# Attention value products as four 64x64 array tiles into two PSUM banks, with row sums of the second key tiles by accumulating DMAs

## The chip, the cores and the metric

The kernel runs on one core of one Trainium2 chip. The metric is device time in microseconds (us) of that core; the times below are medians over runs of the same kernel. The trace and the page come from one further execution, taken by the hardware profiler.

Engine names: PE is TensorE, DVE is VectorE, ACT is ScalarE, POOL is GpSimd, SP is SyncE. PEld stands for weight loads, which overlap with matmuls. L1001 is line 1001 of the kernel before.

## The reference

Two images of 64 channels and 96 x 96 pixels go through a convolution stage and a one-head attention over all N = 9216 pixels; nearly all of the time is spent in the second.

```python
h = group_norm1(x, n1_g, n1_b)
f = dwconv(h, w3, b3) + dwconv(h, w5, b5) + dwconv(h, w7, b7)
g = sigmoid(conv1x1(f, gate_w, gate_b))
x = x + conv1x1(f * g, proj_w, proj_b)
h = group_norm1(x, n2_g, n2_b)
q = conv1x1(h, q_w, q_b).reshape(B, C, N).transpose(0, 2, 1)
k = conv1x1(h, k_w, k_b).reshape(B, C, N)
v = conv1x1(h, v_w, v_b).reshape(B, C, N).transpose(0, 2, 1)
attn = softmax(einsum('bnc,bcm->bnm', q, k) * C ** -0.5, axis=-1)
out = einsum('bnm,bmc->bnc', attn, v)
return x + out.transpose(0, 2, 1).reshape(B, C, H, W)
```

## The kernel before

Per image the queries are cut into 18 blocks (j) of 512. A block goes over 72 tiles of 128 keys, taken as 36 pairs (p = 0 to 35, the two tiles of a pair are t = 0 and 1). For a pair, `scores` (L980) makes two 128x512 score tiles in two PSUM banks, from fp16 parts with 64 rows and 128 columns of weights at a time, so that two such products use the two halves of the array's rows. One ScalarE instruction (`exponentials`, L540) turns both tiles into exponentials in slot p of the ring E in SBUF, 8 pairs deep. `weigh` (L997) multiplies them by the values: 128 rows and 64 columns of fp32 weights per key tile, tile t = 0 into the upper 64 partitions of one bank (ACC_BANK, 6) and t = 1 into the lower 64. Each fp32 matmul is two records in the trace, one per pass over the 512 columns.

The softmax needs the sum of the exponentials per query. GpSimd adds up the first tiles of the pairs in accA (`add_a`, L466); VectorE adds up the second tiles in PSUM bank 7 (`add_b`, L800) and copies them out to accB at the block's end (`sums_out`). In the next block GpSimd adds accA and accB (`total`, L479), TensorE sums over partitions (`row_sums`, L1033), ScalarE copies the sums out, VectorE takes reciprocals in eight parts, GpSimd adds the two halves of the value products (pva, pvb), multiplies them by the reciprocals, and VectorE adds the residual (`write_out`). The value products are moved out of PSUM by three ScalarE copies of 64x256 (`move_pv`, L551, behind the exponentials of p = 1) and one VectorE copy (`move_last_pv`, L825, the first thing in a VectorE block).

The softmax also needs a bound of each row's maximum, for the block after: `visit` (L1049) makes maximum scores into two PSUM banks (MX_BANK) twice per two pairs, and VectorE reduces each to one column (`reduce_max`, L787), which frees the banks for the next visit. Near the block's end the maxima are spread over partitions by TensorE (`spread_maxima`, L1012), placed by ScalarE (`place_maxima`), and turned by GpSimd into a source, mseed (`fill_source`, L487, the first thing in a GpSimd block); `seed` (L578) on ScalarE then writes mseed into the score banks of every odd pair from 3 on, two pairs ahead, and the scores of that pair accumulate on it.

Every engine has one queue, in the order of the code, and waits for counting semaphores. On TensorE two pairs go in this order: visit(p), scores of p + 2, scores of p + 3 (behind the seed), visit(p + 1), weigh(p), weigh(p + 1). The row sums of the block before stand between weigh(6) and weigh(7), the spread of maxima between weigh(32) and weigh(33). The two score tiles of an even pair and of an odd pair each have their own two banks.

## Time and profile before

| | us |
|---|---|
| median of 2 runs | 2826.18 (2825.94 to 2826.41) |
| span of the profiled execution | 2823.7 |
| TensorE busy | 2759.1 (98%) |
| VectorE busy | 2501.6 (89%) |
| ScalarE busy | 2207.9 (78%) |
| GpSimd busy | 1823.3 (65%) |
| share of the 16 DMA engines, hardware queues | 6.1% |

The profile gives the busy time of an engine as the union of its instructions. Ends of matmuls are modelled and overlap the next start, so that the pace of TensorE is read from starts. The timeline merges neighbouring instructions of one line into one row with a count; a row's second number is the time from the first start to the last end.

### The profile page before, as it was taken

The numbers are of one execution on the slowest core, as the hardware profiler recorded it, in microseconds if no ns is written. First come the engines' busy times: TensorE is split into PE (matmuls) and PEld (weight loads), VectorE is DVE, ScalarE is ACT, GpSimd is POOL, SyncE is SP. The second block draws the span as 40 slices with busy tenths as digits, with TensorE's granted clock in tenths as the row PEclk, the third lists the DMA queues.
The fourth block names the chain that finished last, engine by engine and source line by source line (L and its number), as shares of the span: only waits on it lengthen the run. The fifth ranks groups of instructions, "written<-read, shape, count | busy, mean of one in ns | idle before, by whom it ended". The sixth has DMA issues, their size and how long they took to land.

```text
span 2823.7 us, 54475 instructions
## 1 busy us (share of the span) xinstructions
PE 2759.1 (98%) x19648; PEld 935.0 (33%) x19648; DVE 2501.6 (89%) x3164; ACT 2207.9 (78%) x2290; POOL 1823.3 (65%) x1479
## 2 busy tenths in 40 slices
PE   7899999999999999999988999999999999999999
PEld 4333333333333333333323333333333333333332
DVE  5689999999999999999758999999999999999994
ACT  4467888888888888888867788888888888888888
POOL 1346666666666666666754666666666666666666
PEclk9999999999999999999999999999999999999999
DMA  6103000000000000000000000000000000000000
GB/s 203 41 9 75 10 11 10 11 10 10 11 10 11 10 11 11 10 11 9 5 5 16 9 10 11 10 11 11 11 10 10 11 10 11 10 10 9 9 7 5
DMA packets 35768, 48.20 MB, mean 17 GB/s; under 512 B 7848, under 2 KB 33960, under 8 KB 34992
## 3 DMA queue, kind: packets, MB, share of 16 engines
q1 hardware_dynamic: 35504, 44.75, 6.1%
q8 instruction: 157, 2.57, 0.4%
q14 instruction: 107, 0.88, 0.1%
HBM read 16.41 MB, written 9.44 MB: 9 GB/s over the span
## 4 chain that ended last, share of the span: by engine, by line
PE 93%; DVE 4%; issue 1%; ACT 1%; POOL 0%; SPq 0%; DMA 0%; DVEq 0%; ACTq 0%; POOLq 0%
PE ps L1001 42%; PE ps L992 35%; PE ps L1008 12%; DVE mxp L791 3%; PE ps L1121 2%; PE ps L1036 1%; PE ps L1207 0%; PE ps L1148 0%; PE ps L1163 0%; DVE ps L807 0%; PE ps L1097 0%; PE ps L1017 0%; ACT arena L547 0%; DVE bn L898 0%; ACT ps L583 0%
## 5 line engine op out<-in xcount | busy, mean ns | idle before, releaser
L471 POOL TENSOR_TENSOR arena<-arena 128x512 f32<-128x512 f32 x1224 | 1558.8, 1274 | 792.6 <-ACT arena L547 713.7
L791 DVE TENSOR_REDUCE mxp<-ps 128x1 f32<-128x1024 f32 x1296 | 1575.5, 1220 | 171.6 <-PE ps L1008 139.9
L547 ACT ACTIVATE arena<-ps,bnd 128x1024 f32<-128x1024 f32 x1296 | 1372.7, 1110 | 416.0 <-PE ps L992 362.0
L1001 PE MATMUL ps<-arena,vals 128*64 128x512 f32 x5184 | 1268.2, 605 | 0.2
L992 PE MATMUL ps<-arena 64*128 64x512 f16 x7776 | 1051.8, 376 | 5.3 <-ACT ps L583 3.2
L807 DVE TENSOR_TENSOR ps<-ps,arena 128x512 f32<-128x512 f32 x1224 | 844.8, 690 | 68.1 <-ACT arena L547 67.3
L583 ACT ACTIVATE ps<-mseed 128x1024 f32<-128x1024 f32 x612 | 629.0, 1028 | 56.5 <-ACT arena L547 4.8
L1008 PE MATMUL ps<-arena,QM 64*128 64x512 f16 x2592 | 500.0, 383 | 18.2 <-DVE mxp L791 13.5
L992 PEld LDWEIGHTS ps<-arena 64*128 64x128 f16 x7776 | 375.2, 94 | 419.6 <-ACT arena L547 28.8
L1001 PEld LDWEIGHTS ps<-arena,vals 128*64 128x64 f32 x5184 | 310.8, 136 | 501.6 <-issue 337.5
L1008 PEld LDWEIGHTS ps<-arena,QM 64*128 64x128 f16 x2592 | 124.6, 93 | 738.8 <-DVE mxp L791 638.5
L992 PE MATMUL ps<-arena,one 64*128 64x512 f16 x1368 | 259.6, 376 | 0.0
L823 DVE RECIPROCAL rec<-rsum 128x32 f32<-128x32 f32 x280 | 95.2, 342 | 0.1
L992 PEld LDWEIGHTS ps<-arena,one 64*128 64x128 f16 x1368 | 66.7, 94 | 81.0
L490 POOL TENSOR_SCALAR mseed<-arena 128x512 f32<-128x512 f16 x36 | 53.6, 1490 | 34.2 <-ACT arena L576 31.4
L476 POOL TENSOR_TENSOR arena<-arena 128x512 f32<-128x512 f32 x36 | 45.9, 1274 | 35.0 <-ACT arena L547 35.0
L1121 PE MATMUL ps<-arena 32*24 32x384 f32 x1792 | 56.0, 540 | 12.5 <-issue 6.3
L524 POOL TENSOR_TENSOR arena<-arena 128x512 f16<-128x512 f32 x36 | 41.7, 1161 | 37.3 <-ACT arena L671 37.3
L1207 PE MATMUL ps<-f,wT 128*128 128x512 f32 x72 | 43.2, 698 | 4.9 <-ACT f L653 3.2
L485 POOL TENSOR_TENSOR accS<-arena 128x512 f32<-128x512 f32 x35 | 45.4, 1296 | 0.1
L638 ACT ACTIVATE arena<-ps,prm 128x512 f32<-128x512 f32 x18 | 12.3, 687 | 40.8 <-PE ps L1148 40.8
L514 POOL TENSOR_TENSOR f<-f,arena 128x512 f32<-128x512 f32 x18 | 22.7, 1273 | 32.7 <-ACT arena L638 32.7
(122 smaller groups left out, 667.4 us busy)
## 6 DMA issues: line engine op xcount, KB each, us to landing
arena<-arena SPq DMA_DIRECT2D x144, 64.0 KB, 2.0
arena<-in_x_rows SPq DMA_DIRECT2D x8, 816.0 KB, 9.8
xs<-in_x SPq DMA_DIRECT2D x4, 1152.0 KB, 15.6
f_scratch<-arena SPq DMA_DIRECT2D x32, 144.0 KB
f<-f_scratch SPq DMA_DIRECT2D x16, 288.0 KB, 9.9
QM<-arena SPq DMA_DIRECT2D x72, 64.0 KB, 2.0
xst<-arena SPq DMA_DIRECT2D x72, 64.0 KB, 1.9
out<-ot SPq DMA_DIRECT2D x72, 64.0 KB, 2.0
```

The costliest lines, as they stand in the source:

```text
L471: nc.gpsimd.tensor_tensor(accA[:, n % 2, :], accA[:, n % 2, :], e, ALU.add).then_inc(adda_free, 1)
L476: nc.gpsimd.tensor_tensor(accA[:, n % 2, :], E[:, slot_of(n % 2, 0), 0, :], E[:, slot_of(n % 2, 1), 0, :], ALU.add).then_inc(adda_free, 2)
L490: nc.gpsimd.tensor_scalar(mseed[:, n % 2, :], QS[:, n % 2, 2, :], ONE * C, None, ALU.mult).then_inc(mseed_ready, 1)
L547: nc.scalar.activation(flat(E[:, slot_of(n % 2, p), :, :]), flat(ps[:, S_BANK + 2 * buf:S_BANK + 2 * buf + 2, :]), ACT.Exp, scale=bnd[:, 6 ...
L583: nc.scalar.activation(ps[:, S_BANK + 2:S_BANK + 4, :], mseed[:, n % 2, :].unsqueeze(1).to_broadcast([P, 2, CH]), ACT.Copy).then_inc(seede ...
L791: nc.vector.reduce_max(flat(mxp[:])[:, v:v + 1], flat(ps[:, bank:bank + 2, :]), AX.X).then_inc(mx_free, 1)
L807: nc.vector.tensor_tensor(ps[:, SUM_BANK, :], ps[:, SUM_BANK, :], e, ALU.add).then_inc(addb_free, 1)
L823: nc.vector.reciprocal(rec[:, at], rsum[:, at]).then_inc(rec_ready, 1)
L992: a = nc.tensor.matmul(ps[:, S_BANK + 2 * (p % 2) + t, :], of[rows], QS[rows, par, part, :], start=(k == 0 and seeds is None), stop=(k == ...
L1001: a = nc.tensor.matmul(ps[C * t:C * t + C, ACC_BANK, :], V[:, p, t, :], E[:, slot_of(par, p), t, :], start=(p == 0), stop=(p == NPAIR - 1) ...
L1008: a = nc.tensor.matmul(ps[:, bank + t, :], QM[rows, half, qt * P:(qt + 1) * P], KH[rows, kc * CH:(kc + 1) * CH], start=True, stop=True)
L1121: a = nc.tensor.matmul(ps[GRP * h:GRP * h + WROWS, conv_bank(s) + g, 0:WN].rearrange("p (w x) -> p w x", x=W), bands[rows, k * KW + dx, :] ...
```

## The change

- `weigh` makes four products per pair instead of two: the 128 keys of a tile are split into two halves of 64 rows (r), so that each product has 64 rows and 64 columns. The halves r go to two banks, 6 and 7, and are added later.
- Bank 7 is therefore no longer free for the sums of second tiles. In blocks 0 to 16 of an image GpSimd issues 18 DMAs (`dump`), each of two pairs' second tiles (128 partitions x 1024 fp32, 512 KB), into two halves of accD in turn: the first of each half copies, the others add to what is there (`accum_op`). A dump waits on GpSimd's queue for the one two before it to have landed. They stand behind the adds of the pairs in DUMP_AFTER, the last two both behind p = 35. In block 17 VectorE still adds, in bank 4.
- VectorE adds accD together behind p = 6 of the next block (`sum_dumps`: one add of 128x1024, one of 128x512).
- The ring E has 12 pairs instead of 8, laid out so that second tiles of neighbouring pairs are contiguous. The exponential of a pair waits for the dump of the pair 12 earlier instead of for VectorE's add.
- The value products leave PSUM so: one ScalarE copy of 128x512 from bank 6 (`move_pv`, behind p = 1), one VectorE add of bank 7 to it (`add_pv`, first in VectorE's block), two ScalarE copies of 64x256 across partitions (`turn_pv`, behind p = 4), two VectorE adds of 64x256 (`sum_pv`, behind p = 10, instead of GpSimd's add).
- The row sums move from p = 6 to p = 12, GpSimd's total from the block's start to behind p = 8, its final product from p = 28 to 33, the reciprocals to p = 17 to 31, `write_out` from p = 32 to 35.

```diff
-NSLOT = 8
+NSLOT = 12
-ROW_SUMS = 6
+ROW_SUMS = 12
+LASTS = NBLK - 1
+DUMP_AFTER = (8, 9, 11, 12, 14, 15, 17, 18, 20, 21, 23, 25, 27, 29, 31, 33, 35, 35)
+NDUMP = len(DUMP_AFTER)
+DUMPS_SUMMED = 6
...
+            def dump(b, j, g):
+                n, k = blk(b, j), g % 2
+                at = slot_of(n % 2, 2 * g)
+                pool.wait_ge(e_ready, NPAIR * n + 2 * g + 3)
+                if g >= 2:
+                    pool.wait_ge(dumped[k], dumps_before(b, j, g))
+                    pool.dma_start(accD[:, k, :], E[:, 1, at:at + 2, :].rearrange("p s c -> p (s c)"), accum_op=ALU.add
+                                   ).then_inc(dumped[k], 16)
+                else:
+                    if n:
+                        pool.wait_ge(accb_out, n)
+                    pool.dma_start(accD[:, k, :], E[:, 1, at:at + 2, :].rearrange("p s c -> p (s c)")).then_inc(dumped[k], 16)
...
                 fill_source(n)
                 first_a(n)
-                if j:
-                    total(n - 1)
                 for p in range(2, NPAIR):
                     add_a(n, p)
-                    if j and p == 12:
-                        pool.wait_ge(acc_free, 4 * n)
-                        if n > 1:
-                            pool.wait_ge(o_ready, n)
-                        nc.gpsimd.tensor_tensor(pvt[:], pva[:], pvb[:], ALU.add).then_inc(pv_summed, 1)
-                    if j and p == 28:
+                    if j < LASTS:
+                        for g in range(NDUMP):
+                            if DUMP_AFTER[g] == p:
+                                dump(b, j, g)
+                    if j and p == DUMPS_SUMMED + 2:
+                        total(n - 1)
+                    if j and p == 33:
                         pool.wait_ge(rec_ready, RECS * n)
...
                 act.wait_ge(adda_free, m + 1)
-                act.wait_ge(addb_free, m + 1)
-                nc.scalar.activation(flat(E[:, slot_of(n % 2, p), :, :]),
-                                     flat(ps[:, S_BANK + 2 * buf:S_BANK + 2 * buf + 2, :]),
+                if m >= NSLOT:
+                    was, q = divmod(m - NSLOT, NPAIR)
+                    b, j = divmod(was, NBLK)
+                    if j < LASTS:
+                        act.wait_ge(dumped[q // 2 % 2], dumps_before(b, j, q // 2) + 16)
+                    else:
+                        act.wait_ge(addb_free, NPAIR * b + q + 1)
+                nc.scalar.activation(E[:, :, slot_of(n % 2, p), :],
+                                     ps[:, S_BANK + 2 * buf:S_BANK + 2 * buf + 2, :],
...
-                for k, h in parts:
-                    nc.scalar.activation((pva, pvb)[k][C * h:C * h + C, :],
-                                         ps[C * k:C * k + C, ACC_BANK, h * HCH:(h + 1) * HCH], ACT.Copy).then_inc(acc_free, 1)
+                nc.scalar.activation(flat(pvc[:]), ps[:, ACC_BANK, :], ACT.Copy).then_inc(acc_copied, 1)
+
+            def turn_pv(n):
+                act.wait_ge(acc_free, n + 1)
+                for h in (0, 1):
+                    nc.scalar.activation(pvx[C * h:C * h + C, :], pvc[C - C * h:2 * C - C * h, h, :], ACT.Copy).then_inc(pv_turned, 1)
...
+            def sum_dumps(b, j):
+                n = blk(b, j)
+                for k in (0, 1):
+                    dve.wait_ge(dumped[k], dumps_before(b, j + 1, 0))
+                chain(nc.vector.tensor_tensor(accD[:, 0, :], accD[:, 0, :], accD[:, 1, :], ALU.add))
+                if n:
+                    dve.wait_ge(sum_ready, n)
+                nc.vector.tensor_tensor(accB[:], accD[:, 0, 0:CH], accD[:, 0, CH:2 * CH], ALU.add).then_inc(accb_out, 1)
...
-                nc.vector.tensor_copy(pvb[C:P, :], ps[C:P, ACC_BANK, HCH:CH]).then_inc(acc_free, 1)
+            def add_pv(n):
+                dve.wait_ge(acc_copied, n + 1)
+                nc.vector.tensor_tensor(flat(pvc[:]), ps[:, ACC_BANK + 1, :], flat(pvc[:]), ALU.add).then_inc(acc_free, 1)
...
-                    if p + 1 < NPAIR:
-                        add_b(n, p + 1)
+                    if j == LASTS and p + 1 < NPAIR:
+                        add_b(b, n, p + 1)
+                    if j and p == 10:
+                        sum_pv(n - 1)
+                    if j and p == DUMPS_SUMMED:
+                        sum_dumps(b, j - 1)
...
                 for t in (0, 1):
-                    a = nc.tensor.matmul(ps[C * t:C * t + C, ACC_BANK, :], V[:, p, t, :], E[:, slot_of(par, p), t, :],
-                                         start=(p == 0), stop=(p == NPAIR - 1), skip_group_check=True)
+                    for r in (0, 1):
+                        rows = slice(C * r, C * r + C)
+                        a = nc.tensor.matmul(ps[C * t:C * t + C, ACC_BANK + r, :], V[rows, p, t, :],
+                                             E[rows, t, slot_of(par, p), :], start=(p == 0), stop=(p == NPAIR - 1),
+                                             skip_group_check=True)
...
                     if p == 0 and not first:
-                        pe.wait_ge(acc_free, 4 * n)
+                        pe.wait_ge(acc_free, n)
```

## Rows read from the trace of the kernel before

**Rows 1.** The page: its first line, and the chain that ended last by engine.
```profile
span 2823.7 us, 54475 instructions
...
PE 93%; DVE 4%; issue 1%; ACT 1%; POOL 0%; SPq 0%; DMA 0%; DVEq 0%; ACTq 0%; POOLq 0%
```

**Rows 2.** Timeline, a steady period: start us, length us, engine, line, operation, count.
```profile
703.13 1.94 PE L1001 MATMUL ps<-arena,vals 128*64 128x512 f32 x8
...
703.57 2.69 POOL L471 TENSOR_TENSOR arena<-arena 128x512 f32<-128x512 f32 x2 [1.23 <-ACT arena L547]
...
704.59 1.03 ACT L583 ACTIVATE ps<-mseed 128x1024 f32<-128x1024 f32 x1
...
705.00 0.39 PE L1008 MATMUL ps<-arena,QM 64*128 64x512 f16 x2
...
705.43 1.23 DVE L791 TENSOR_REDUCE mxp<-ps 128x1 f32<-128x1024 f32 x1
...
705.87 0.38 PE L992 MATMUL ps<-arena,one 64*128 64x512 f16 x2
...
706.74 0.38 PE L1008 MATMUL ps<-arena,QM 64*128 64x512 f16 x2
...
707.05 1.51 PE L1001 MATMUL ps<-arena,vals 128*64 128x512 f32 x6
```

**Rows 3.** Timeline of TensorE around the row sums of two neighbouring blocks.
```profile
687.94 0.60 PE L1036 MATMUL ps<-accS,ones 128*64 128x256 f32 x4
...
759.13 0.60 PE L1001 MATMUL ps<-arena,vals 128*64 128x512 f32 x2
759.56 0.60 PE L1036 MATMUL ps<-accS,ones 128*64 128x256 f32 x4
```

**Rows 4.** Timeline of TensorE, one stretch of the convolution, 16 array tiles.
```profile
83.32 0.92 PE L1121 MATMUL ps<-arena 32*24 32x384 f32 x32
```

**Rows 5.** Timeline of TensorE between the images, three array shapes in turn.
```profile
1450.75 0.60 PE L1001 MATMUL ps<-arena,vals 128*64 128x512 f32 x2
1451.28 1.98 PE L1148 MATMUL ps<-f,wT 128*128 128x512 f32 x4
1453.19 0.65 PE L1036 MATMUL ps<-accS,ones 128*64 128x256 f32 x4
```

**Rows 6.** The page's groups: count, busy us, mean ns, idle before and its releaser.
```profile
L807 DVE TENSOR_TENSOR ps<-ps,arena 128x512 f32<-128x512 f32 x1224 | 844.8, 690 | 68.1 <-ACT arena L547 67.3
...
L485 POOL TENSOR_TENSOR accS<-arena 128x512 f32<-128x512 f32 x35 | 45.4, 1296 | 0.1
```

**Rows 7.** Timeline around a block's boundary.
```profile
739.78 0.60 ACT L576 ACTIVATE arena<-ps 128x512 f16<-128x512 f32 x1
...
741.68 1.49 POOL L490 TENSOR_SCALAR mseed<-arena 128x512 f32<-128x512 f16 x1
...
744.04 1.03 ACT L583 ACTIVATE ps<-mseed 128x1024 f32<-128x1024 f32 x1
...
744.84 0.43 DVE L830 COPY pvb<-ps 64x256 f32<-64x256 f32 x1
...
745.00 0.76 ACT L556 ACTIVATE pva<-ps 64x256 f32<-64x256 f32 x2
...
746.58 0.39 PE L1008 MATMUL ps<-arena,QM 64*128 64x512 f16 x2
```

**Rows 8.** Timeline of SP's queue: two DMAs issued.
```profile
741.07 1.12 SPq L363 DMA_DIRECT2D QM<-arena  x2
```

**Rows 9.** Groups of GpSimd by line, columns as in the page's groups.
```profile
L508 POOL TENSOR_TENSOR pvt<-pvt,rec 128x256 f32<-128x256 f32 x34 | 24.9, 732 | 0.0
```

**Rows 10.** The page's DMA issues: count, KB each, median us to landing.
```profile
arena<-in_x_rows SPq DMA_DIRECT2D x8, 816.0 KB, 9.8
...
QM<-arena SPq DMA_DIRECT2D x72, 64.0 KB, 2.0
```

**Rows 11.** Windows: busy us of each engine, TensorE's clock, DMA share, GB/s.
```profile
10.00:30.00 20.00, 13.73 (x217) 9.28 (x210) 9.45 (x31) 14.81 (x20) 0.00 (x0) 1.00 1.06 309
```

More of the change, by code:

```diff
@@ L147, in program @@
         accS = sb("accS", [P, CH])
-        pva = sb("pva", [P, HCH])
-        pvb = sb("pvb", [P, HCH])
+        accD = sb("accD", [P, 2, 2 * CH])
+        pvc = sb("pvc", [P, 2, HCH])
+        pvx = sb("pvx", [P, HCH])
         pvt = sb("pvt", [P, HCH])
@@ L237, in program @@
         accb_out = sem("accb_out")
+        dumped = [sem("dumped0"), sem("dumped1")]
         sum_ready = sem("sum_ready")
@@ L242, in program @@
         pv_summed = sem("pv_summed")
+        acc_copied = sem("acc_copied")
         acc_free = sem("acc_free")
+        pv_turned = sem("pv_turned")
         xst_ready = [sem("xst_ready0"), sem("xst_ready1")]
@@ L292, in pair0, with dumps_before @@
             return NPAIR * blk(b, j)
+        def dumps_before(b, j, g):
+            return 16 * (NDUMP // 2 * (LASTS * b + j) + g // 2)
         block = ctx.enter_context(nc.Block())
@@ L526, in _ @@
                     attend(b, j)
-                n = blk(b, NBLK - 1)
                 if b + 1 < B:
-                    total(n)
-                else:
-                    pool.wait_ge(acc_free, 4 * (n + 1))
-                    pool.wait_ge(o_ready, n + 1)
-                    nc.gpsimd.tensor_tensor(pvt[:], pva[:], pvb[:], ALU.add).then_inc(pv_summed, 1)
+                    total(blk(b, NBLK - 1))
         @block.scalar
@@ L594, in attend @@
                     if p == 1 and j:
-                        move_pv(n - 1, ((0, 0), (0, 1)))
-                        act.wait_ge(acc_free, 4 * n - 1)
-                        move_pv(n - 1, ((1, 0),))
+                        move_pv(n - 1)
+                    if p == 4 and j:
+                        turn_pv(n - 1)
                     if p == NPAIR - 3 and j + 1 < NBLK:
@@ L639, in _ @@
                                          bias=prm[:, GB:GB + 1]).then_inc(sig_ready, 1)
-                    if b and c in (1, 2):
-                        move_pv(blk(b, 0) - 1, ((c - 1, 0), (c - 1, 1)))
+                    if b and c == 1:
+                        move_pv(blk(b, 0) - 1)
+                    if b and c == 4:
+                        turn_pv(blk(b, 0) - 1)
                     if b and c == 3:
@@ L677, in _ @@
                     move_pv(blk(b, NBLK - 1))
+                    turn_pv(blk(b, NBLK - 1))
         @block.vector
@@ L853, in attend @@
                 if j:
-                    move_last_pv(n - 1)
+                    add_pv(n - 1)
                 for p in range(NPAIR):
@@ L872, in attend @@
                     if j:
-                        if 11 <= p < 11 + 2 * RECS and p % 2:
-                            reciprocals(n - 1, (p - 11) // 2)
-                        if p == 32:
+                        if ROW_SUMS + 5 <= p < ROW_SUMS + 5 + 2 * RECS and p % 2:
+                            reciprocals(n - 1, (p - ROW_SUMS - 5) // 2)
+                        if p == 35:
                             write_out(b, j - 1)
-                sums_out(n)
+                if j == LASTS:
+                    sums_out(b, n)
             joint_kernel()
@@ L910, in _ @@
                         x1_stats(c - 1)
+                    if b and c == 2:
+                        add_pv(blk(b, 0) - 1)
                     if b and c in (4, 5):
@@ L959, in _ @@
             n = blk(B - 1, NBLK - 1)
+            add_pv(n)
+            sum_pv(n)
             dve.wait_ge(rs_ready, n + 1)
```

46 lines of the change are left out of this document (22 added, 24 removed).

## The prediction

> **What bounds the kernel now.** I read the page first: the span, and the chain that ended last. 93% of that chain is TensorE [rows 1]: the span is a queue of matmuls, and work on other engines counts only where a matmul waits for it.
>
> Next the timeline of a steady stretch [rows 2]. One period treats two pairs of key tiles and lasts 707.05 - 703.13 = 3.92 us. TensorE goes without a pause from the value products (L1001) to maximum scores A (L1008, 705.00), scores (L992), maximum scores B (706.74) and value products again. The other engines have slack, but not everywhere:
> - VectorE's maximum over A runs from 705.43 to 706.66, and B, which overwrites the same two banks, starts at 706.74. Whatever delays that maximum, or stands long on VectorE between it and the next one, stops TensorE.
> - ScalarE's seed ends at 705.62; it is needed by the second half of the scores, which starts at 705.87. Slack 0.25 us.
> - GpSimd spends 2.69 us of 3.92 on its two adds, 1.345 us a pair against a pace of 1.96.
>
> Then one whole block of 36 pairs: from one block's row-sum matmuls to the next, 759.56 - 687.94 = 71.62 us [rows 3]. 18 x 3.92 = 70.56 of it is steady, so today's block boundary costs about 1 us. Of the 36 blocks 34 issue dumps, and 34 begin behind a block of the same image.
>
> **What the four tiles do.** The same 512 columns pass the array twice per matmul; today the two 64-column halves run side by side, 0.43 us a pass, 759.13 to 759.56 [rows 3]. Quarter tiles need the same passes if all four run side by side. The convolution says they do: 32 records of 16 tiles, two passes each, fit in 0.92 us [rows 4]. So the passes themselves gain nothing.
>
> What could be gained is the change of array shape. In each period L1001's four passes take 1.87 us up to 705.00, which is 4 x 0.43 + 0.15, and B to L1001 takes 0.31 where a plain pass takes (706.74 - 705.00) / 8 = 0.22 [rows 2]: about 0.25 us in all. I read it as 0.10 at each change and 0.05 for a first weight load: L1036 takes 0.65 us behind a change of shape and 0.60 without one [rows 3, 5]. Today rows (64 to 128) and columns (128 to 64) both change; afterwards only columns do. The trace has changes of columns alone, back to back [rows 5]: from L1001 (128x64) to L1148 (128x128) a pass takes 0.53 instead of 0.43, and L1148's four passes before L1036 (128x64) take 1.91, 0.19 over 4 x 0.43 for a change and a first weight load. So a change of columns alone costs 0.10 too, and I take the gain as 0, bounds 0 and 0.25 us a period (4.5 us a block).
> No row shows the pair 64x128 to 64x64 itself. The Trainium skill (TensorEngine Tiling (Array Packing), Tiling Modes) says that a change of tiling mode, unlike a change of tile, drains the engine, and lists 64x128 and 64x64 as different modes; by it the gain is 0.
>
> Two insertions get worse. Row sums and the spread of maxima stay 128x64 and today stand inside value products without a gap. Now each is a change to and fro: 2 x (2 x 0.10 + 2 x 0.05 for first loads) = **0.6 us a block** (below: 0, if changes of rows alone were free).
>
> **VectorE.** It loses 34 x 34 of its adds on L807, 0.69 us each [rows 6]. As TensorE does not wait for them, that gives 0. It gets sum_dumps after the maximum of p = 6, which is an A: a 128x1024 add and, behind a semaphore, a 128x512 add. No such add is in the trace; by the maximum over 1024 [rows 2] and L807 they take 1.23 + 0.06 + 0.69. The next maximum would end near 705.00 + 4.7, where the next A wants it by 3.92: **0.8 us a block** (below: 0, were the dumps' sum slid into slack). Two 64x256 adds after p = 10, under 0.9 us by the 0.43 of L830 [rows 7], fit where the old add was.
>
> **ScalarE.** turn_pv, two 64x256 copies (0.76 us, as the two of L556 [rows 7]), stands after p = 4, between two exponentials and ahead of the next seed. 0.76 against 0.25 of slack: **0.5 us a block** (bounds 0, if the exponentials can start earlier, and 0.8).
>
> **GpSimd and the boundary.** This is the largest term. 18 dumps a block are new on GpSimd's queue. The trace has no DMA from GpSimd; X is the time for which one holds it. SP issues two halves of 64 partitions in 1.12 us [rows 8]; a dump covers 128 partitions, so I take X = 1.12. Bounds: 0.56, one issue, below (0, were it all off the engine), and above 1.4, an estimate: a quarter more, since the target is also read.
> The Trainium skill (DMA: Bandwidth & Descriptors, Latency and other measured facts) has about 1 us to the first byte from GpSimd against about 0.6 from SP. By X = 1.0 the time would be 3,014 us.
>
> From p = 8 to 35 GpSimd has 28 adds x 1.345 = 37.7, the total (1.3) and the final product (0.7) [rows 6, 9] and 16 dumps before the last two: 39.7 + 16 X against 28 x 1.96 = 54.9. It ends the block late by 16 X - 15.2 = 2.7 us. Then two dumps, both after p = 35, stand ahead of the next block's fill_source: 2 X = 2.2. The last dump waits for the one two before it to land. A 64 KB transfer lands in 2.0 us [rows 10] and the loads at the start move 309 GB/s [rows 11], so 512 KB lands in about 3.7, or 5.4 if reading the target doubles it; GpSimd does 4.9 us of other work meanwhile: 0 to 0.5, taken as 0.3.
> So fill_source ends 5.3 us later than the 743.17 of today, L490 [rows 7], and the seed behind it, today at 744.04, waits. What is late next: seed 1.03, then the new move_pv (128x512, 0.60 as L576), then add_pv on VectorE (0.69), which stands ahead of the maximum over A (1.23), which B needs. With hops of about 0.05 B starts 3.8 us after fill_source ends; today it starts at 746.58. TensorE stops for 743.17 + 5.3 + 3.8 - 746.58 = **5.7 us a block**. If fill_source were not late at all, the longer chain alone (move_pv after the seed that ends at 745.07, then add_pv, where today L830 takes 0.43 beside ScalarE's copies) puts B at 747.7: 1.1 us, the bound below.
> The ring grows from 8 to 12 pairs, so the exponential's wait for a dump, issued four to eleven pairs ahead (7.8 us or more), is covered by a landing of under 5.4 us; with that cover gone TensorE would stop here too (second rival).
>
> **Sum.** 0.6 + 0.8 + 0.5 + 5.7 = 7.6 us, x 34 = 258 us. At the end of the program two copies and an add become a chain, about 2 us, and as much between the images. 2823.7 + 258 + 4 = 3,086 for the span; the median of the runs lies 2.5 above the profiled span: 3,088 us. With X = 0.56: (0.6 + 0.8 + 0.5 + 1.8) x 34 = 126, 2,956 us; with X = 1.4: 12.6 x 34 = 428, 3,258 us.
>
> **Rivals.**
> *The change of shape disappears*, because rows stay split in two. For it: only columns differ now. Against it: [rows 5]. It gives 36 x 4.5 = 162 us back. With X = 0.56: 2826 - 162 + 130 = 2,794 us, no change by 2%. But a faster TensorE leaves GpSimd 28 x 1.835 = 51.4 us, so that it is late from X = 0.73 on; at X = 1.12 the time is near 3,040. It decides (not slower by 2%) below X = 0.85; to be faster by over 2% the charges at p = 4 and 6 must be hidden as well.
> *The accumulating transfers are the bound.* 18 of them in 54.9 us on two chains allow a landing of 6.1 us each. The 816 KB loads, many at a time, land in 9.8 [rows 10]; at 9.8 the block would grow by 9 x 9.8 - 54.9 = 33 us, some 3,950 us; at 7 by 8 us and the 1.9 of the other terms, about 3,170.
> *The four tiles don't run together.* The passes would double: 18 x 1.72 x 36 = 1,115 us, about 3,940 us. Against it: [rows 4].
> *The boundary is better hidden than I count*: X near 0 and sum_dumps in slack: (0.6 + 1.1 + 0.5) x 34 = 75, 2,905 us.
>
> **How the numbers follow.** Forecast 0.56; shape change gone 0.14; transfers the bound 0.13; tiles not together 0.03; boundary hidden 0.14. The predicted time is the forecast's. The range takes in X from 0.56 to 1.4, the hidden boundary and the first rival at X = 0.56, and leaves out its faster part, most of the transfer case and the doubled passes: 2,790 to 3,280 us. A measurement of this kernel tells about 2%. Faster by over 2%: half of the first rival, 0.07. Within 2%: a part of the same rival and of the hidden case, 0.13. Slower: 0.80.
>
> **What the profile would show.** Right: L1001's passes at 0.43 us in groups of four tiles, with 0.10 still at each change; gaps on both sides of the row sums; GpSimd's L490 late and the seed waiting for it; TensorE idle some 5 us before the second maximum scores of each block, released by the maximum behind add_pv; a shorter stop after p = 6. Wrong: a steady period of 3.67 us; L490 as early as now; a dump that GpSimd is done with in 0.3 us; exponentials waiting for transfers.

## The result

| | before | after |
|---|---|---|
| median, us | 2826.18 (2825.94 to 2826.41) | 3034.35 (3020.39 and 3048.30) |
| span of the profiled execution, us | 2823.7 | 3046.6 |
| TensorE busy | 2759.1 (98%) | 2835.0 (93%) |
| VectorE busy | 2501.6 (89%) | 1956.6 (64%) |
| GpSimd busy | 1823.3 (65%) | 2302.1 (76%) |
| a block, us (median) | 71.61 (28 blocks) | 76.75 (12 blocks at full clock); 78.42 (16 blocks with a stretch of half clock) |

The blocks are the second to the fifteenth of each image. The changed kernel is slower: the ratio of the times is 1.0737 with a 95% interval of 1.062 to 1.0854. The forecast was 3,088 us, in a range of 2,790 to 3,280.

Lines of the changed kernel: value products L1058, maximum scores L1066, scores L1047, row sums L1094, maximum L827, exponentials L576, seed L617, fill_source L519, move_pv L585, add_pv L874, turn_pv L591, sum_dumps L850 and L853, GpSimd's adds L486, dumps L506 (plain) and L501 (accumulating). In the experiments they are shifted by a few lines.

The page of after: first line, busy time, and the chain that ended last by engine (compare [rows 1]).

```profile
span 3046.6 us, 63708 instructions
...
PE 2835.0 (93%) x24832; PEld 948.9 (31%) x24832; DVE 1956.6 (64%) x2081; ACT 2218.5 (73%) x2288; POOL 2302.1 (76%) x2056
...
PE 69%; DVE 10%; POOL 7%; issue 6%; ACT 6%; DMA 1%; ACTq 0%; SPq 0%; POOLq 0%; DVEq 0%
```

VectorE has lost more than a fifth of its work, and yet its share of the chain has grown from 4% to 10%; TensorE's has fallen from 93% to 69%. Where VectorE stands now counts more than how much it does.

Timeline of before, the first maximum scores at the two ends of a boundary period and of a period with row sums.

```profile
744.67 0.39 PE L1008 MATMUL ps<-arena,QM 64*128 64x512 f16 x2
...
748.77 0.39 PE L1008 MATMUL ps<-arena,QM 64*128 64x512 f16 x2
...
756.60 0.39 PE L1008 MATMUL ps<-arena,QM 64*128 64x512 f16 x2
...
760.95 0.39 PE L1008 MATMUL ps<-arena,QM 64*128 64x512 f16 x2
```

They take 748.77 - 744.67 = 4.10 us and 760.95 - 756.60 = 4.35 us.

Timeline of after, TensorE in one steady period and around the row sums (start us, length us, engine, line; compare [rows 2, 3]).

```profile
502.29 0.39 PE L1066 MATMUL ps<-arena,QM 64*128 64x512 f16 x2
...
504.33 1.95 PE L1058 MATMUL ps<-arena,vals 64*64 64x512 f32 x16
...
506.21 0.39 PE L1066 MATMUL ps<-arena,QM 64*128 64x512 f16 x2
...
509.28 0.65 PE L1094 MATMUL ps<-accS,ones 128*64 128x256 f32 x4
...
510.88 0.39 PE L1066 MATMUL ps<-arena,QM 64*128 64x512 f16 x2
```

The steady period is 506.21 - 502.29 = 3.92 us, as before. Sixteen records of quarter tiles take 1.95 us, as eight records of two tiles took: all four run side by side, and nothing is gained. The period with the row sums is 510.88 - 506.21 = 4.67 us.

Timeline of after around the boundary of [rows 7] (in brackets: idle before, and what ended it).

```profile
474.92 0.88 POOL L501 DMA_DIRECT2D accD<-arena  x1
...
476.04 0.87 POOL L501 DMA_DIRECT2D accD<-arena  x1 [0.24 <-issue]
...
476.99 1.49 POOL L519 TENSOR_SCALAR mseed<-arena 128x512 f32<-128x512 f16 x1
...
478.14 0.39 PE L1066 MATMUL ps<-arena,QM 64*128 64x512 f16 x2
...
478.51 1.03 ACT L617 ACTIVATE ps<-mseed 128x1024 f32<-128x1024 f32 x1 [1.09 <-POOL mseed L519]
...
479.47 0.58 ACT L585 ACTIVATE pvc<-ps 128x512 f32<-128x512 f32 x1
...
480.08 0.69 DVE L874 TENSOR_TENSOR pvc<-ps,pvc 128x512 f32<-128x512 f32 x1 [2.09 <-ACT pvc L585]
480.69 1.21 DVE L827 TENSOR_REDUCE mxp<-ps 128x1 f32<-128x1024 f32 x1
...
481.96 0.39 PE L1066 MATMUL ps<-arena,QM 64*128 64x512 f16 x2 [1.46 <-DVE mxp L827]
...
484.16 0.39 PE L1066 MATMUL ps<-arena,QM 64*128 64x512 f16 x2
```

This is the forecast's chain, link by link: dumps, fill_source, seed, move_pv, add_pv, maximum, second maximum scores. The period lasts 484.16 - 478.14 = 6.02 us. The wait ahead of the last dump, 0.24 here, is for the dump two before it to land: the last dump starts 0.56 us behind that landing in 30 of the 34 blocks. In 11 of the 34 blocks it is 0.8 to 1.7 us, in nine of them because that transfer landed 5.4 to 6.3 us after its issue instead of 4.8, and fill_source and the stop come later by about as much.

Timeline of after behind p = 4 and p = 6.

```profile
486.59 0.86 ACT L591 ACTIVATE pvx<-pvc 64x256 f32<-64x256 f32 x2
...
489.85 0.82 PE L1047 MATMUL ps<-arena 64*128 64x512 f16 x6 [0.51 <-ACT ps L617]
...
494.27 1.22 DVE L850 TENSOR_TENSOR accD<-accD 128x1024 f32<-128x1024 f32 x1
...
495.19 1.43 POOL L486 TENSOR_TENSOR arena<-arena 128x512 f32<-128x512 f32 x1 [1.68 <-ACT arena L576]
...
495.52 1.65 DVE L853 TENSOR_TENSOR arena<-accD 128x512 f32<-128x512 f32 x1
...
498.36 0.39 PE L1066 MATMUL ps<-arena,QM 64*128 64x512 f16 x2 [1.67 <-DVE mxp L827]
```

turn_pv makes the seed late. sum_dumps' second add, 128x512, takes 1.65 us beside an add of GpSimd, where L807 of the same size took 0.69 [rows 6]; TensorE then stands for 1.67 us.

The page's groups and DMA issues of after (count, busy us, mean ns; KB each, median us to landing), and two of its waits (in total, times, longest).

```profile
L501 POOL DMA_DIRECT2D accD<-arena x544 | 496.8, 914 | 34.9 <-ACT arena L576 11.4
...
L506 POOL DMA_DIRECT2D accD<-arena x68 | 40.9, 602 | 36.6 <-DVE arena L853 36.6
...
accD<-arena POOLq DMA_DIRECT2D x612, 512.0 KB, 4.8
...
POOL arena L486 <- ACT arena L576: 422.9, 444, 5.8
...
ACT arena L576 <- DMA accD<-arena: 4.7, 2, 4.0
```

One thing the forecast didn't have: behind many of the boundary stops TensorE's clock is half. Timeline of after in a later block, then windows over the same stretch (busy us of each engine, granted clock, DMA share, GB/s).

```profile
713.04 0.39 PE L1066 MATMUL ps<-arena,QM 64*128 64x512 f16 x2 [1.46 <-DVE mxp L827]
713.36 3.59 PE L1058 MATMUL ps<-arena,vals 64*64 64x512 f32 x16
```

```profile
709.50:713.30 3.80, 1.19 (x10) 0.35 (x8) 1.82 (x2) 3.62 (x5) 2.41 (x3) 1.00 0.95 194
713.40:716.60 3.20, 3.20 (x18) 0.76 (x16) 1.22 (x1) 0.86 (x1) 1.35 (x2) 0.50 0.10 27
716.90:720.80 3.90, 3.90 (x38) 1.28 (x34) 2.45 (x2) 2.55 (x4) 1.27 (x1) 1.00 0.00 0
```

Behind 3.80 us in which TensorE worked for 1.19, the granted clock is 0.50, that is 1.2 instead of 2.4 GHz, and the sixteen products take 3.59 us instead of 1.95. (In this block the last dump waited for 1.01 us, so that its stop is 0.9 us longer than the one shown above.) The page's span has 25 such stretches against 5 before; 16 of the 28 blocks of the first table have one.

**Where a block's time went.** The table takes each block apart by the starts of its first maximum scores: 18 periods a block, medians over blocks with full clock, us.

| period with | before | after | difference |
|---|---|---|---|
| the boundary | 4.10 | 6.03 | +1.93 |
| turn_pv (p = 4) | 3.92 | 4.62 | +0.70 |
| sum_dumps (p = 6) | 3.92 | 5.66 | +1.74 |
| the row sums | 4.35 | 4.67 | +0.32 |
| the spread of maxima | 4.20 | 4.49 | +0.29 |
| the 13 others, together | 51.12 | 51.28 | +0.16 |
| block | 71.61 | 76.75 | +5.14 |

5.14 x 34 = 175 us. The 20 additional half-clock stretches at about 1.67 (78.42 - 76.75) are 33. That is 208 of the 223 us between the spans. About 11 more are the longer stops of the blocks whose last dump waited longer; the rest lies in blocks with longer half-clock stretches, in the block during which the second image is loaded, and at the ends.

### The profile page after: what moved, and what is told of

The parts are those of the page before. It is cut to its first block, busy times and chain, and to the rows that moved or that the text cites. A ratio compares the mean times of both kernels' runs of the same rounds, so it can differ in the third digit from the quotient of the medians.

```text
span 3046.6 us, 63708 instructions
## 1 busy us (share of the span) xinstructions
PE 2835.0 (93%) x24832; PEld 948.9 (31%) x24832; DVE 1956.6 (64%) x2081; ACT 2218.5 (73%) x2288; POOL 2302.1 (76%) x2056
## 4 chain that ended last, share of the span: by engine, by line
PE 69%; DVE 10%; POOL 7%; issue 6%; ACT 6%; DMA 1%; ACTq 0%; SPq 0%; POOLq 0%; DVEq 0%
PE ps L1058 31%; PE ps L1047 24%; PE ps L1066 9%; DVE mxp L827 6%; POOL arena L486 3%; ACT arena L576 3%; DVE arena L853 2%; POOL mseed L519 2%; PE ps L1179 2%; ACT ps L617 1%; DVE accD L850 1%; POOL accD L501 1%; DMA accD<-arena 1%; ACT pvx L591 1%; DVE pvc L874 1%
## 5 line engine op out<-in xcount | busy, mean ns | idle before, releaser
L827 DVE TENSOR_REDUCE mxp<-ps 128x1 f32<-128x1024 f32 x1296 | 1579.9, 1223 | 857.6 <-PE ps L1066 856.5
L486 POOL TENSOR_TENSOR arena<-arena 128x512 f32<-128x512 f32 x1224 | 1642.3, 1342 | 490.0 <-ACT arena L576 422.9
L576 ACT ACTIVATE arena<-ps,bnd 128x1024 f32<-128x1024 f32 x1296 | 1379.5, 1111 | 571.0 <-PE ps L1047 559.2
L1058 PE MATMUL ps<-arena,vals 64*64 64x512 f32 x10368 | 1310.1, 616 | 0.6 <-DVE pvc L874 0.6
L1047 PE MATMUL ps<-arena 64*128 64x512 f16 x7776 | 1054.8, 377 | 49.5 <-ACT ps L617 45.9
L617 ACT ACTIVATE ps<-mseed 128x1024 f32<-128x1024 f32 x612 | 628.9, 1028 | 101.1 <-POOL mseed L519 50.1
L1066 PE MATMUL ps<-arena,QM 64*128 64x512 f16 x2592 | 503.7, 385 | 117.7 <-DVE mxp L827 113.0
L501 POOL DMA_DIRECT2D accD<-arena x544 | 496.8, 914 | 34.9 <-ACT arena L576 11.4
L1047 PEld LDWEIGHTS ps<-arena 64*128 64x128 f16 x7776 | 373.6, 94 | 480.1 <-issue 96.1
L1058 PEld LDWEIGHTS ps<-arena,vals 64*64 64x64 f32 x10368 | 330.8, 134 | 522.4 <-issue 356.4
L1066 PEld LDWEIGHTS ps<-arena,QM 64*128 64x128 f16 x2592 | 125.3, 93 | 847.0 <-DVE mxp L827 686.0
L1047 PE MATMUL ps<-arena,one 64*128 64x512 f16 x1368 | 259.9, 376 | 0.0
L1047 PEld LDWEIGHTS ps<-arena,one 64*128 64x128 f16 x1368 | 66.8, 94 | 81.5 <-issue 0.8
L843 DVE TENSOR_TENSOR ps<-ps,arena 128x512 f32<-128x512 f32 x68 | 47.6, 699 | 59.4 <-ACT arena L576 57.8
L874 DVE TENSOR_TENSOR pvc<-ps,pvc 128x512 f32<-128x512 f32 x36 | 24.9, 691 | 91.9 <-ACT pvc L585 91.9
L519 POOL TENSOR_SCALAR mseed<-arena 128x512 f32<-128x512 f16 x36 | 54.4, 1512 | 33.8 <-ACT arena L610 31.4
L506 POOL DMA_DIRECT2D accD<-arena x68 | 40.9, 602 | 36.6 <-DVE arena L853 36.6
L853 DVE TENSOR_TENSOR arena<-accD 128x512 f32<-128x512 f32 x34 | 54.2, 1593 | 1.2
L491 POOL TENSOR_TENSOR arena<-arena 128x512 f32<-128x512 f32 x36 | 45.6, 1266 | 6.7 <-ACT arena L576 3.9
```

Of the source, the lines that this page charges most:

```text
L486: nc.gpsimd.tensor_tensor(accA[:, n % 2, :], accA[:, n % 2, :], e, ALU.add).then_inc(adda_free, 1)
L501: pool.dma_start(accD[:, k, :], E[:, 1, at:at + 2, :].rearrange("p s c -> p (s c)"), accum_op=ALU.add).then_inc(dumped[k], 16)
L519: nc.gpsimd.tensor_scalar(mseed[:, n % 2, :], QS[:, n % 2, 2, :], ONE * C, None, ALU.mult).then_inc(mseed_ready, 1)
L576: nc.scalar.activation(E[:, :, slot_of(n % 2, p), :], ps[:, S_BANK + 2 * buf:S_BANK + 2 * buf + 2, :], ACT.Exp, scale=bnd[:, 6:7]).then_in ...
L617: nc.scalar.activation(ps[:, S_BANK + 2:S_BANK + 4, :], mseed[:, n % 2, :].unsqueeze(1).to_broadcast([P, 2, CH]), ACT.Copy).then_inc(seede ...
L827: nc.vector.reduce_max(flat(mxp[:])[:, v:v + 1], flat(ps[:, bank:bank + 2, :]), AX.X).then_inc(mx_free, 1)
```

## The experiments

Theory: the tiles give TensorE nothing, and the loss is a sum of places where another engine's new work makes TensorE wait. Rivals: the tiles do gain, and the stops hide it; or the load of the transfers, or of GpSimd, is what costs, wherever the work stands.

### Two tiles again

```diff
-                    for r in (0, 1):
-                        a = nc.tensor.matmul(ps[C * t:C * t + C, ACC_BANK + r, :], V[rows, p, t, :],
+                    a = nc.tensor.matmul(ps[C * t:C * t + C, ACC_BANK, :], V[:, p, t, :],
...
-                nc.vector.tensor_tensor(flat(pvc[:]), ps[:, ACC_BANK + 1, :], flat(pvc[:]), ALU.add).then_inc(acc_free, 1)
+                nc.vector.tensor_tensor(flat(pvc[:]), ps[:, ACC_BANK, :], flat(pvc[:]), ALU.max).then_inc(acc_free, 1)
```

> The kernel after, with the value products back as two 128x64 tiles into bank 6; add_pv takes a maximum of bank 6 with its own copy, so that its wait and its cost stay. Theory (the change of shape costs the same for 64x64 tiles, so the tiles give the steady period nothing and only make the two insertions of 128x64 products dearer): steady period 3.92 us as now, the periods with the row sums and the spread of maxima 0.3 and 0.5 us shorter, 0.85 us a block, 36 blocks, some 30 us below the kernel after: about 3,005 us. Rival (four tiles gain something that the new stops hide): the steady period grows to about 4.1 us and the time stays or rises. Rival (quarter tiles are themselves slower, by loads or by writing two banks): the steady period falls below 3.9 and the time by 60 us or more.

Measured: 3035.27 us (3032.51 to 3039.27), 1.0744 of before. The steady period stays 3.92; the row sums and the spread are 4.35 and 4.20 again, to the digit those of before. But the boundary grows from 6.03 to 6.32: the 0.29 saved just ahead of it is waited out there, since GpSimd's queue comes no earlier. A block is 76.28, so 0.47 less, and the span has 27 half-clock stretches. The 30 us that the theory expected don't show, and the times can't tell the two kernels apart; the periods can, and they bear out that the tiles give the steady period nothing.

### fill_source first

```diff
                 fill_source(n)
+                if j:
+                    for g in (NDUMP - 2, NDUMP - 1):
+                        dump(b, j - 1, g)
                 first_a(n)
```

> The kernel after, with the last two dumps of a block moved behind fill_source of the next block. Theory (fill_source is late by two dumps of 0.88 us on GpSimd's queue, and the seed, move_pv, add_pv and the maximum wait in a row behind it): fill_source ends up to 1.75 us earlier, the first cycle of a block falls from about 6.0 to about 5.0 us (the longer chain move_pv, add_pv stays), about 1 us a block, 34 us; and if the half-clock stretches that follow the boundary stop are caused by its length, most of them go too, another 0 to 40 us: 2,960 to 3,000 us. Rival (the chain move_pv, add_pv alone makes the stop, fill_source was in time): the first cycle stays near 6.0 and the time near 3,030 us. Rival (the transfers themselves load the memory): the same, no change.

Measured: 2967.26 us (2967.11 to 2968.72), 1.0506 of before. Timeline of this kernel's boundary:

```profile
474.23 1.49 POOL L519 TENSOR_SCALAR mseed<-arena 128x512 f32<-128x512 f16 x1
...
475.78 1.81 POOL L501 DMA_DIRECT2D accD<-arena  x2
...
476.68 1.03 ACT L620 ACTIVATE ps<-mseed 128x1024 f32<-128x1024 f32 x1
...
477.32 0.39 PE L1069 MATMUL ps<-arena,QM 64*128 64x512 f16 x2
...
480.14 0.39 PE L1069 MATMUL ps<-arena,QM 64*128 64x512 f16 x2 [0.92 <-DVE mxp L830]
```

fill_source now starts 3.09 us ahead of the first maximum scores instead of 1.15, and the seed waits for nothing. The boundary takes 5.02 us: 1.01 of its 1.93 was the two dumps ahead of fill_source, 0.92 is the longer chain through move_pv and add_pv. And 6 half-clock stretches are left in the whole span, about as many as before. So a move that shortens one stop by 1 us gave 67 us, and 80 between the two spans: 34 from the stop, some 32 from 19 half-clock stretches less, and about 11 from the last dump's longer waits, which now stand behind fill_source.

### turn_pv behind the seeds

```diff
-                    if p == 4 and j:
-                        turn_pv(n - 1)
+                    if p in (5, 7) and j:
+                        turn_pv(n - 1, ((p - 5) // 2,))
```

> The kernel after, with turn_pv's two copies moved from between the exponentials and the seed of p = 4, 5 to behind the seeds of p = 5 and p = 7, one each, where ScalarE is idle for 0.68 us. Theory (the copies make the seed late): the third cycle of a block falls from 4.62 to 3.93 us, 0.7 us a block, 24 us less: about 3,010 us. Rival (the work only moves and stops the array one period later, since ScalarE has no room): 0 to 5 us.

Measured: 3007.92 us (3004.00 to 3012.30), 1.0646 of before. The period of 4.62 is 3.93, a block 76.05, and no other period moved: as forecast. The span has 21 half-clock stretches.

### sum_dumps in three

```diff
-                    if j and p == DUMPS_SUMMED:
-                        sum_dumps(b, j - 1)
+                    if j and p in (DUMPS_SUMMED - 4, DUMPS_SUMMED - 2, DUMPS_SUMMED):
+                        sum_dumps(b, j - 1, (p - DUMPS_SUMMED + 4) // 2)
```

> The kernel after, with sum_dumps cut into three adds of 128x512, one each behind the maxima over A of p = 2, 4 and 6, where GpSimd runs no add. Theory (two adds in a row hold VectorE past the next maximum, and the second, 1.65 us beside a GpSimd add instead of 0.69, suffers from what the two engines share): each add takes about 0.7 us, the cycle of 5.66 us falls to 3.93, 1.7 us a block, 58 us less: about 2,975 us. Rival (the add is slow for its operands, whoever runs beside it): each of the three takes 1.2 to 1.65 us, three cycles of about 4.3 us take the place of the one, and the gain is 0.6 us a block, 20 us.

Measured: 3075.79 us (3072.55 to 3078.02), 1.089 of before: slower than the changed kernel. Timeline behind p = 6 and p = 10:

```profile
496.40 0.68 DVE L856 TENSOR_TENSOR arena<-accD 128x512 f32<-128x512 f32 x1
...
503.63 1.27 POOL L486 TENSOR_TENSOR arena<-arena 128x512 f32<-128x512 f32 x1
...
504.25 3.08 DVE L884 TENSOR_TENSOR pvt<-pvc,pvx 64x256 f32<-64x256 f32 x2
...
505.48 1.56 POOL L486 TENSOR_TENSOR arena<-arena 128x512 f32<-128x512 f32 x1
...
507.37 1.22 DVE L827 TENSOR_REDUCE mxp<-ps 128x1 f32<-128x1024 f32 x1
508.65 0.39 PE L1069 MATMUL ps<-arena,QM 64*128 64x512 f16 x2 [1.98 <-DVE mxp L827]
```

The three adds take 0.68, 0.82 (median over both lines of L852) and 0.68 us, and the period of 5.66 is 3.93: that part is as the theory has it, and the operands alone are not slow. But without the stop at p = 6 GpSimd stands elsewhere in its order when VectorE reaches sum_pv behind p = 10. sum_pv's two adds of 64x256, 0.99 us together in after, take 3.08: the first ends at 505.17, 0.27 behind GpSimd's add that began at 503.63, the second 0.29 behind the one that ended at 507.04. TensorE stands for 1.98 us; this period is now 5.97, and behind it the clock is half in 21 of the 31 blocks that have this stop (43 half-clock stretches in the span). The loss has moved, as the rival says, but to the next pair of adds that meet.

### The moves together, sum_pv clear of GpSimd's adds

```diff
-DUMP_AFTER = (8, 9, 11, 12, 14, 15, 17, 18, 20, 21, 23, 25, 27, 29, 31, 33, 35, 35)
+DUMP_AFTER = (9, 10, 11, 12, 14, 15, 17, 18, 20, 21, 23, 25, 27, 29, 31, 33, 35, 35)
...
-                    if j and p == DUMPS_SUMMED + 2:
+                    if j and p == DUMPS_SUMMED + 4:
                         total(n - 1)
...
-                    if j and p == 10:
+                    if j and p == 8:
                         sum_pv(n - 1)
```

besides the three edits above.

> The kernel after with the three moves together (last dumps behind fill_source; turn_pv behind the seeds of p = 5 and 7; sum_dumps as three adds behind p = 2, 4, 6), and sum_pv from behind p = 10 to behind p = 8, with the first two dumps and GpSimd's total one to two adds later, so that no GpSimd add runs beside sum_pv. Theory (the loss is a sum of places where one engine's new work makes TensorE wait, and two-operand adds of VectorE stand still while a GpSimd add or dump runs): periods of 3.93 us at turn_pv, sum_dumps and sum_pv, 5.02 at the boundary, 4.67 and 4.49 at the two insertions of 128x64 products; block 73.2 to 73.5 us against 71.6 before, no half-clock stretches: about 2,885 us. Rival (the load of the transfers or of GpSimd as such, whose stop turns up somewhere else as it did when sum_dumps alone was moved): a block of 75 us or more, over 2,940 us.

Measured: 2907.42 us (2903.38 to 2908.84), 1.0289 of before. The block is 73.30 us, with 3.93 at turn_pv, sum_dumps and sum_pv, 5.02 at the boundary, 4.67 and 4.49 at the insertions: every period is the theory's, and 6 half-clock stretches remain. The time is 22 us above it. Timeline of this kernel in the block during which SyncE loads the second image:

```profile
249.49 1.22 SPq L340 DMA_DIRECT2D f<-f_scratch  x2
...
265.22 0.69 DVE L855 TENSOR_TENSOR accD<-accD 128x512 f32<-128x512 f32 x1 [13.76 <-DMA accD<-arena]
```

That block takes 89.70 us, 16.4 more than the others, because VectorE waits 13.76 us for dumps to land while the loads are under way, which makes one period 13.5 us longer, and the next is 2.9 longer at half clock (that the loads are the cause is read from the time alone; it wasn't tried apart); the other blocks are 0.25 above their median on average, 7 us in all. 57 + 16 + 7 = 80 of the 82 us over before. So the transfers do cost something, in waits for their landing.

### The tiles alone

```diff
-                    a = nc.tensor.matmul(ps[C * t:C * t + C, ACC_BANK, :], V[:, p, t, :], E[:, slot_of(par, p), t, :],
+                    for r in (0, 1):
+                        rows = slice(C * r, C * r + C)
+                        a = nc.tensor.matmul(ps[C * t:C * t + C, ACC_BANK + r, :], V[rows, p, t, :],
...
-                    if p + 1 < NPAIR:
-                        add_b(n, p + 1)
```

in the kernel before.

> The kernel before with its value products as four 64x64 tiles into banks 6 and 7 and nothing else of the change. It leaves out the sums of the second key tiles (accB is zero) and the half of the value products that lands in bank 7. Theory (a change between 64x128 and 64x64 tiles costs what a change from 64x128 to 128x64 does): steady period 3.92 us, row sums and spread of maxima 0.3 us dearer each, 36 x 0.6 = 22 us: about 2,848 us. Rival (with rows always split in two the array's change is free, and the change of the kernel would have paid but for what it brings along): steady period 3.67 us, about 2,685 us. Rival (VectorE's adds, which are gone here, held TensorE up after all): below 2,826 us at a steady period of 3.92.

Measured: 2848.87 us (2848.00 to 2850.26), 1.0085 of before. Timeline of TensorE, the value products' period and the one with the row sums:

```profile
467.56 0.39 PE L1007 MATMUL ps<-arena,QM 64*128 64x512 f16 x2
...
471.48 0.39 PE L1007 MATMUL ps<-arena,QM 64*128 64x512 f16 x2
...
474.55 0.65 PE L1035 MATMUL ps<-accS,ones 128*64 128x256 f32 x4
...
476.15 0.39 PE L1007 MATMUL ps<-arena,QM 64*128 64x512 f16 x2
```

3.92 and 4.67 us, the same as in after. The block is 72.35, 0.74 above before: 0.61 in the insertions, the rest in 0.007 a period. With no dumps, no sum_dumps, no longer chain, and with VectorE rid of its adds, the four tiles make the kernel slower by 0.85%.

### All products as 64x64

```diff
-                    for t in (0, 1):
-                        a = nc.tensor.matmul(ps[:, S_BANK + 2 * (p % 2) + t, :], of[rows], QS[rows, par, part, :],
+                    for h in (0, 1):
+                        for t in (0, 1):
+                            rows, to = slice(C * t, C * t + C), slice(C * h, C * h + C)
+                            a = nc.tensor.matmul(ps[to, S_BANK + 2 * (p % 2) + t, :], of[rows, to], QS[rows, par, part, :],
```

and the same in max_scores, on top of the tiles alone.

> As the run with the four tiles alone (the same is left out), with scores and maximum scores as 64x64 tiles too: each 64x128 weight is two of 64 columns, into the two halves of the same bank. No product of the steady period changes the array's shape any more. Theory (the 0.10 us belong to the change of columns): steady period about 3.67 us, 36 x 18 x 0.25 = 162 us less than with the tiles alone: about 2,690 us. Rival (the 0.10 us belong to the change between fp16 and fp32 or between weights): steady period 3.92, about 2,848 us. Rival (twice as many weight loads don't hide): a steady period above 3.92 and more than 2,850 us.

Measured: 2704.34 us (2701.26 to 2706.48), 0.9574 of before. Timeline of TensorE:

```profile
451.86 0.41 PE L1010 MATMUL ps<-arena,QM 64*64 64x512 f16 x4
...
453.84 1.89 PE L1000 MATMUL ps<-arena,vals 64*64 64x512 f32 x16
...
455.56 0.39 PE L1010 MATMUL ps<-arena,QM 64*64 64x512 f16 x4
```

This period is 3.70 us, most are 3.67: 0.25 less, the whole amount that the two changes of shape were read to cost. The value products' four passes take 455.56 - 453.84 = 1.72 us, 4 x 0.43 with nothing added. It is the columns that cost, not the change from fp16 to fp32, and twice as many weight loads hide.

### The same in the whole kernel

On top of the moves together, scores and maximum scores as 64x64 tiles.

> The kernel with the moves together, and scores and maximum scores as 64x64 tiles: it computes all. Theory: the steady period loses the two changes of shape, 0.25 us, 162 us in all: 2,885 - 162 = 2,723 us, if GpSimd keeps up; its 35 adds of 1.345, 18 dumps of 0.9, total, product and source are 66.8 us of a block of 68.8, so that it may end a block late by up to 2.7 us: 2,723 to 2,815 us, below the kernel before. Rival (the shape is not what costs, or the loads don't hide): 2,885 us or more.

Measured: 2906.63 us (2897.57 to 2914.07), 1.0294 of before: no better than with 64x128 scores. The steady period is 3.67, but the boundary is back. The waits of this kernel (engine and line, released by; us in total, times, longest):

```profile
ACT ps L620 <- POOL mseed L519: 69.7, 32, 3.6
```

GpSimd ends each block late, its fill_source too; VectorE's first add of the dumps' sum also waits, 32.8 us in total, for dumps to land; and the span has 28 half-clock stretches. The theory named GpSimd's lateness, and its price was put too low: the time lies above the whole of its range.

### The boundary without GpSimd

```diff
+                act.wait_ge(m_ready, n + 1)
+                nc.scalar.activation(mseed[:, n % 2, :], QS[:, n % 2, 2, :], ACT.Copy, scale=ONE * C).then_inc(mseed_ready, 1)
...
-                if j:
-                    add_pv(n - 1)
                 for p in range(NPAIR):
...
+                    if j and p == 0:
+                        add_pv(n - 1)
```

on top of the moves together, add_pv behind the maximum of p = 0.

> The kernel with the moves together, with two more moves at the boundary: ScalarE fills mseed itself, behind place_maxima where it stands idle for 1.6 us, instead of GpSimd's fill_source; and add_pv stands behind the block's first maximum instead of ahead of it. Theory (the 0.9 us by which the boundary is still longer than before is the chain seed, move_pv, add_pv, maximum, ahead of the second maximum scores): with the maximum in front, the second maximum scores start on time and only the first value products wait for add_pv; the boundary period falls from 5.02 to 4.1 to 4.3 us, the block from 73.3 to about 72.5, 27 us less than the kernel with the moves together (2,907 us): about 2,880 us. What is left over the kernel before is then the two insertions (0.6 us a block) and the transfers of the second image. Rival (the first value products wait for add_pv as long as the second maximum scores did): the boundary stays near 5.0 and the time near 2,905 us.

Measured: 2871.30 us (2869.95 to 2874.45), 1.0171 of before. The boundary takes 4.19 us, the block 72.46. The 0.85 a block left over before are the insertions' 0.61, 0.09 at the boundary and 0.15 in the steady periods; times 34 that is 29 of the 47 us, and 7 more are the block with the loads. Of the other 11, eight blocks with one longer period make 4; the rest is not assigned.

And the same with all products of the steady period as 64x64:

> As the run before it, with scores and maximum scores as 64x64 tiles; it computes all. Theory (in the 64x64 version before this one GpSimd had the work, ended each block late, and the boundary waited for its fill_source): with no work of GpSimd left in the boundary's chain its lateness is taken up by the ring of 12 pairs; steady period 3.67 us, boundary about 4, block about 68.3 to 69.5, 2,880 - 162 = 2,718 to 2,760 us, below the kernel before by 2.5 to 4%. Rival (GpSimd, with 65.6 us of work in a block of 68, is the bound wherever the boundary's work stands, and VectorE's two-operand adds run into it): exponentials wait for GpSimd, block over 71 us, 2,820 us or more.

Measured: 2888.88 us (2871.49 to 2896.60), 1.0212 of before. The boundary is 4.08 as meant, but the first add of the dumps' sum now stands on VectorE's queue until the last dumps have landed. Timeline of this kernel:

```profile
472.24 1.19 DVE L851 TENSOR_TENSOR accD<-accD 128x512 f32<-128x512 f32 x1 [3.57 <-DMA accD<-arena]
```

In the third to the sixteenth block of each image this period takes 5.8 to 8.7 us, 7.3 at the median, and the span has 30 half-clock stretches.

### The sum one period later

```diff
-                    for k in (0, 1):
-                        dve.wait_ge(dumped[k], dumps_before(b, j + 1, 0))
+                dve.wait_ge(dumped[part > 0], dumps_before(b, j + 1, 0))
...
-DUMPS_SUMMED = 6
+DUMPS_SUMMED = 8
```

accB now takes the first accumulator's two parts, then the second's, one each; turn_pv and sum_pv moved as the expectation says. The next block's first dump waits for the first of these adds only, no longer for all; what the two changes are worth apart wasn't tried.

> The 64x64 version of before with the sum of the dumps one period later: its three adds of 128x512 behind the maxima of p = 4, 6 and 8, the first of them waiting for one of the two last dumps only; turn_pv behind the seeds of p = 3 and 5, sum_pv's halves behind the adds of p = 6 and 8. Theory (in the version before it the add behind p = 2 stood on VectorE's queue waiting 3.6 us for the last dumps, which a late GpSimd issues and which then need 4.7 us to land; the maximum behind it was late, and the clock fell): the wait is gone, periods of 3.67 us but for the insertions and some 0.25 us at p = 6 and 8; block 68.5 to 70 us, 2,735 to 2,780 us, below the kernel before by 2 to 3%. Rival (GpSimd falls further back until something else waits for it, the exponentials or the next dumps): a block of 71 us or more, 2,820 us and more.

Measured: 2761.26 us (2760.81 to 2764.55), 0.9776 of before, with an interval of 0.9759 to 0.9792: the only version that computes all and is faster than before. The block is 69.37, half-clock stretches are 6 again.

## Why the prediction was right

The time lay 54 us below the forecast, inside the range, and the mechanism was the forecast's. That the number came so close is partly luck: terms too low and a term too high met, and the clock, which the forecast didn't have, made up for a part of the difference.

- **The four tiles gain nothing: right**, and now measured by itself. Passes at 0.43 us, period 3.92, in after and with the tiles alone. The rival that the change of shape disappears falls; the run with all products as 64x64 shows that it does disappear, 0.25 us a period, where columns don't change either. The rule of the Trainium skill (TensorEngine Tiling (Array Packing), Tiling Modes) that a change of mode drains the engine agrees, for a change of columns alone.
- **The two insertions, 0.6 us a block: right**, 0.61 measured, gone to the digit with two tiles.
- **turn_pv, 0.5: too low by 0.2.** The pair of copies took 0.86 us where 0.76 was read from L556 [rows 7]; that is half of the error, the other half is not assigned.
- **sum_dumps, 0.8: too low, 1.74.** The term that failed is the 0.69 for the 128x512 add, read from L807 [rows 6]. L807 has one operand in PSUM; the new add has both in SBUF and ran beside GpSimd's add, 1.65 us. The 0.96 between them is the whole error (0.94).
- **GpSimd and the boundary, 5.7: too high, 1.93.** A dump holds GpSimd for 0.88 us, not 1.12, so that 16 of them are 14.1, under the 15.2 of room: GpSimd isn't late in the block (its adds still wait 422.9 us for exponentials in the span), and 2.7 of the 5.3 us fall away. The rest was right: two dumps and a wait, 2 x 0.88 + 0.24 = 2.0 us. Measured against the first maximum scores, fill_source starts 1.84 later, 478.14 - 476.99 = 1.15 ahead of them instead of 744.67 - 741.68 = 2.99 [rows 7]. B comes 3.48 after fill_source ends (481.96 - 478.48) where 3.8 was worked out. The forecast's own line with these, 743.17 + 1.84 + 3.48 - 746.58, gives 1.91. Of the 5 us of idle time that were to be seen ahead of the second maximum scores, 1.46 are there. The bound below, 1.1, with fill_source on time, was 0.92 in the run that put it first.
- **The landing, 3.7 to 5.4: right**, 4.8, and the rival that the transfers are the bound falls: exponentials waited for them twice in the whole span, 4.7 us in all, 4.0 of it in the block with the second image's loads. The wait of the last dump, taken as 0.3 with 0.5 as the most, was 0.24 in the block shown, but 0.8 to 1.7 in 11 of the 34. That the transfers can matter where the loads of the second image meet them was not seen.
- **Missing: the clock.** Some 33 us or more of the 223 are half-clock stretches behind the boundary stop. The forecast priced a stop at its own length.

With the measured sizes the sum is 0.61 + 1.74 + 0.70 + 1.93 + 0.15 = 5.1 us a block and 175 us, where 258 were forecast; the clock put back some 33 of the 83 us between them.

## What to carry to other kernels

When work is taken off an engine with slack and spread over others, price not its length but where each new piece stands: look for the operation behind it on the same queue, and for who waits for that. Here a change of tile shape paid only when the neighbours on TensorE's queue ended up with the same columns; measure it with everything else left out, as in the run with all products as 64x64. And take the duration of a two-operand operation from a row with the same operands' places and the same neighbour running, not from one of the same size.

## What the runs showed of the hardware

- VectorE's adds with both operands in SBUF and GpSimd's adds held each other up here. The same add of 128x512 took 0.68 us with GpSimd idle and 1.65 beside its add; one of 64x256 took 0.40 or up to 2.14. Adds with one operand in PSUM were not held up: all 1224 of L807 in before took 0.68 to 0.70, though GpSimd's adds ran for more than half of the time. The Trainium skill (SBUF — State Buffer, SBUF: two separate sides) says that the two engines share a pair of ports, which one operation holds to its end, also where a VectorE operation with two SBUF inputs meets a GpSimd operation that reads SBUF. The trace agrees: the adds that came second ended 0.27, 0.29 and 0.55 us behind the end of GpSimd's add, 0.11 to 0.13 less than they take alone. Whether the issue of a dump holds VectorE too, no run here separates.
- A stop of TensorE can cost more than its length. Boundary stops with 1.46 us of idle time in front of the second maximum scores were followed by a stretch at half clock in 16 of 28 blocks, the 1.98 at sum_pv in 21 of 31; none followed the 0.92 of the shortened boundary or the 1.67 at sum_dumps. What decides it among stops of like length stays open.
- Issuing an accumulating DMA of 512 KB held GpSimd for 0.88 us at the median, a plain one of the same size for 0.60; they landed in 4.8 and 3.5 us at the median. In the block with the second image's loads, in the run with the moves together, dumps kept VectorE waiting for 13.8.
